# A fixed list of expert units: 42 of 256 rows, or 31 of 256 rows with 12 of 128 rows

## The reference, cut to what matters

```python
h = x @ down_w + down_b
logits = x @ router_w + router_b - COST_LAMBDA * cost
topv, topi = jax.lax.top_k(softmax(logits), 2)
gate = softmax(topv)
for k in range(2):
    mask = one_hot(topi[..., k], 8)
    acc = 0
    for e, (w1, b1, w2, b2) in enumerate(expert_params):
        hm = h * mask[..., e:e + 1]
        acc = acc + (gelu(gelu(hm) @ w1 + b1) @ w2 + b2)
    out = out + acc * gate[..., k:k + 1]
out = out + 0.1 * shared_expert(h); out = out @ up_w + up_b + gelu(x) @ core_w + core_b
```

## Time and profile before

| | |
|---|---|
| median of 3 runs | 737.02 us (733.06 to 739.28) |
| span of the profiled execution | 740.6 us |
| PE busy | 687.7 us, 93% of the span |
| DVE, ACT, POOL busy | 526.1, 541.0, 479.4 us |
| DMA packets | 123.98 MB |
| expert loop, first to last matmul of a unit | 480.01 to 701.34 us |

### The profile page before, as it was taken

One profiled execution on the slowest core, in us unless ns is written; L12 is line 12 of the kernel. 1 busy time (PEld: TensorE's weight loads), 2 busy tenths in 40 slices (PEclk: granted clock), 3 DMA queues, 4 the chain that ended last, 5 costly groups with the idle time before them and its releaser, 6 DMA issues.

```text
span 740.6 us, 20875 instructions
## 1 busy us (share of the span) xinstructions
PE 687.7 (93%) x6101; PEld 373.9 (50%) x6101; DVE 526.1 (71%) x855; ACT 541.0 (73%) x1129; POOL 479.4 (65%) x474
## 2 busy tenths in 40 slices
PE   1799988999999999999999889799999999999998
PEld 0122222323333333223355444488888888888844
DVE  4999998999999999998887746534444444444456
ACT  2399988999999999999895656376666767676511
POOL 3558788888888888986477142135666656566732
PEclk9999999999999999999999989999999999999999
DMA  6555666566665666545355634489987888887487
GB/s 209 190 157 189 197 195 205 176 201 219 205 193 192 207 208 216 176 139 181 97 170 176 208 117 145 155 169 168 142 123 116 122 121 120 101 109 98 57 268 259
DMA packets 136993, 123.98 MB, mean 167 GB/s; under 512 B 70612, under 2 KB 106452, under 8 KB 136920
## 3 DMA queue, kind: packets, MB, share of 16 engines
q1 hardware_dynamic: 122056, 106.58, 50.7%
q0 software_dynamic: 13632, 15.47, 14.9%
q10 hardware_dynamic: 1232, 0.98, 0.4%
HBM read 60.33 MB, written 51.53 MB: 151 GB/s over the span
## 4 chain that ended last, share of the span: by engine, by line
PE 72%; DVE 9%; DMA 6%; issue 5%; ACT 3%; POOL 2%; SPq 1%; another core or an unknown queue 1%; ACTq 0%; DVEq 0%; POOLq 0%
PE EH L1309 24%; PE Y L1309 16%; PE pv L562 13%; PE ring L549 9%; DVE mx L708 6%; PE nat L537 5%; ACT P L633 2%; DMA k_scratch<-khl 1%; PE ring L581 1%; DVE statx L689 1%; POOL y_sums L2136 1%; PE ring L572 1%; SPq L396 1%; DMA rd<-den_scratch 1%
## 5 line engine op out<-in xcount | busy, mean ns | idle before, releaser
L708 DVE TENSOR_REDUCE mx<-nat 128x2 f32<-128x1024 f32 x256 | 296.7, 1214 | 24.0 <-PE nat L537 23.1
L633 ACT ACTIVATE P<-ring 128x512 f32<-128x512 f32 x512 | 279.4, 603 | 20.4 <-PE ring L549 10.5
L2136 POOL DMA_INDIRECT y_sums<-ysb,to x84 | 138.2, 1645 | 100.5 <-DVE ysb L2070 86.7
L562 PE MATMUL pv<-P,VT 128*32 128x256 f32 x2048 | 159.0, 395 | 0.4
L537 PE MATMUL nat<-KS,QS 48*128 48x512 f16 x512 | 111.7, 397 | 25.7 <-DMA QS<-q_scratch 15.6
L549 PE MATMUL ring<-QS,KS 49*128 49x512 f16 x512 | 123.5, 392 | 8.4 <-ACT P L633 8.4
L1673 ACT ACTIVATE X<-EH,bcur 128x256 f32<-128x256 f32 x168 | 85.6, 560 | 50.5 <-DVE u L2024 26.0
L1309 PE MATMUL Y<-whi,u 128*128 x672 | 117.1, 273 | 0.3 <-DVE u L2024 0.3
L1309 PE MATMUL EH<-XA,whi 128*128 128x256 f16 x672 | 116.9, 273 | 0.3 <-DMA XA<-g_rows 0.3
L2024 DVE TENSOR_TENSOR u<-X,u 128x512 f16<-128x512 f32 x84 | 57.8, 688 | 77.1 <-ACT u L1679 76.4
L1309 PE MATMUL EH<-XA,wlo 128*128 128x256 f16 x336 | 91.6, 273 | 0.0
(11 more groups left out here) (267 smaller groups left out, 985.1 us busy)
## 6 DMA issues: line engine op xcount, KB each, us to landing
XA<-in_wall SPq DMA_DIRECT2D x8, 800.0 KB, 4.4
u<-in_wall SPq DMA_DIRECT2D x8, 800.0 KB, 4.4
QS<-q_scratch SPq DMA_DIRECT2D x64, 96.0 KB, 2.6
KS<-k_scratch SPq DMA_DIRECT2D x62, 96.0 KB, 2.3
X<-in_x SPq DMA_DIRECT2D x16, 256.0 KB, 2.9
q_scratch<-qhl SPq DMA_DIRECT2D x16, 256.0 KB, 2.1
xr<-in_x SPq DMA_DIRECT2D x16, 256.0 KB, 3.6
rd<-den_scratch SPq DMA_DIRECT2D x16, 256.0 KB
```

The source lines that it names most:

```text
L562: m = pe.matmul(pv[32 * j:32 * j + 32, q], VT[i][:, lb, g, j, :], Pb[4 * (s % 2) + j][:, q], start=(lb == 0 and half == 0), stop=(lb == 3) ...
L633: act.activation(Pb[4 * (s % 2) + j][:, :], bank[:, :], ACT.Exp).then_inc(t_use.sem, 1)
L708: dve.tensor_reduce(mx[:, k // 8, :, k % 8], nat[k % 2][:, :, :], AX.X, ALU.max).then_inc(t_max.sem, 1)
L2136: pool.indirect_dma_start(out=ysum[:, :], out_offset=bass.IndirectOffsetOnAxis(ap=to[:, j % 2, a:a + 1], axis=0), in_=ysb[j % 2][:, a, :], ...
```

## The change

The list becomes 31 units of 256 rows and N_HALF = 12 units of 128 rows, NJ = 43; the 12 stand at places 2, 5, 8, ... 35 of the order (SMALL). An expert whose count in 128s is odd has its last 128 rows in a small unit. The tables are looked up over 16 classes (8 experts' odd 128s, then 8 experts' 256s) in place of 8. What isn't needed of the small units is used for pieces of pairs, so that the list still suffices for every distribution. The blank rows behind a count are 128 and not 256.

```diff
-NJ = (2 * ROWS // BLK + E - 1) * 2 - HALVES.count(1)
+N_HALF = sum(HALVES)
+N_FULL = ((2 * ROWS // P + E - 1) * 2 - HALVES.count(1) - N_HALF) // 2
+NJ = N_FULL + N_HALF
+SMALL = [2 + 3 * k for k in range(N_HALF)]
+NCL = 2 * E
...
-    tables = ["nf", "ni", "nb", "H", "c1", "c2", "c3", "ex", "dx", "A", "M1", "r1", "M2", "r2", "pki", "D", "valid",
-              "e", "h", "t", "f", "b", "sub", "ro0", "ro1", "ro2", "ro", "wo0", "wo", "bo0", "bo"]
+    tables = ["ni", "no", "nb", "S", "c1", "c2", "c3", "c4", "ex", "q", "q31", "cv", "cvp", "qh", "qo", "qm", "cd", "yA", "yB", "cp",
+              "A", "M", "r", "valid", "pki", "e", "h", "t", "f", "v", "D", "b", "sub", "ro0", "ro1", "rop", "ro2", "ro",
+              "wo0", "wo", "bo0", "bo"]
...
-                (cur(R_(tables[1:7])) if last else []) + old([("core", 1)]) + (cur(R_(tables[7:])) if last else []) + old([("core", 2)])
+                (cur(R_(tables[1:9])) if last else []) + old([("core", 1)]) + (cur(R_(tables[9:])) if last else []) + old([("core", 2)])
...
-                    sp.dma_start(blocks(region[bass.ds(v, BLK), :]), blank).then_inc(t_zr.sem, 16)
+                    sp.dma_start(region[bass.ds(v, P), :], blank[:, 0, :]).then_inc(t_zr.sem, 16)
...
+            if j in SMALL:                      # hidden
+                g = gS[j % 4]
+                wait(pe, t_act, "E", j - 2, 0)
+                for tile in range(4):
+                    for k in range(2):
+                        wc = bass.ds(v + (C_W1 + tile * LAT + k * P), P)
+                        m = three(EH[j % 2][:, 0, tile * P:(tile + 1) * P], wc, g[:, k, :], g[:, 2 + k, :], k == 0, k == 1)
...
+            if j in SMALL:                      # output
+                wait(pe, t_ah, "E", j, 0)
+                wait(pe, t_dve, "E", j, 0)
+                for tile in range(4):
+                    wc = bass.ds(v + (C_W2 + tile * LAT), LAT)
+                    m = three(EY[j % 2][:, 0, :], wc, ah[j % 2][:, tile, 0:P], al[j % 2][:, tile, 0:P],
+                              tile == 0, tile == 3, swap=True, skip=True)
...
+                if j in SMALL:                  # ScalarE
+                    for tile in range(4):
+                        m = act.activation(af[j % 2][:, tile, 0:P], EH[j % 2][:, 0, tile * P:(tile + 1) * P], ACT.Gelu,
+                                           bias=bcur[:, j % 2, tile:tile + 1], scale=bcur[:, j % 2, 4 + tile:5 + tile])
+                    act.copy(ah[j % 2][:, :, 0:P], af[j % 2][:, :, 0:P]).then_inc(t_ah.sem, 1)
...
+                if j in SMALL:                  # VectorE
+                    dve.tensor_tensor(al[j % 2][:, :, 0:P], af[j % 2][:, :, 0:P], ah[j % 2][:, :, 0:P], ALU.subtract).then_inc(t_dve.sem, 1)
+                    collect(j - 1)
...
-                for a, part in enumerate(("half", "y")):
+                for a, part in enumerate(("half", "y")[0:parts(j)]):
```

More of the change, by code:

```diff
@@ L63 @@
 ROWS = B * D
-REGION = ROWS + BLK
+REGION = ROWS + P
 DUMP = E * REGION
@@ L1077, in ffn @@
     SPLIT = NJ - 2
+    assert all(k < SPLIT for k in SMALL) and N_HALF <= 2 * N_FULL
+    parts = lambda j: 1 if j in SMALL else 2
     def plan_sum(tally, j):
@@ L1087, in ffn @@
         t_mt[j % 4].plan(j)
-        t_ad[j % 2].plan(j, n=2)
-        for n in range(2):
+        t_ad[j % 2].plan(j, n=parts(j))
+        for n in range(parts(j)):
             t_act.plan("E", j, n)
@@ L1280, in rest @@
             assert not xloads
-            wait(sp, t_pe, "E", NJ - 1, "h", 1)
+            wait(sp, t_pe, "E", NJ - 1, "h", parts(NJ - 1) - 1)
             for s in ((NJ - 2) % 2, (NJ - 1) % 2):
@@ L1441, in hidden @@
                 if j >= 2:
-                    wait(pe, t_act, "E", j - 2, n)
+                    wait(pe, t_act, "E", j - 2, min(n, parts(j - 2) - 1))
                 elif n == 0:
@@ L1833, in route @@
             if what == "ex":
-                own("c3")
-                return dve.tensor_tensor(csum[:, :], hc[:, 3, 8:16], hc[:, 0, 8:16], ALU.subtract)
+                own("c4")
+                return dve.tensor_tensor(cx[:, :], hc[:, 2, NCL:2 * NCL], hc[:, 0, NCL:2 * NCL], ALU.subtract)
+            if what == "q":
+                own("c4")
+                return dve.tensor_scalar(qi[:, 0, :], kota, n_tails, 0.0, ALU.subtract, ALU.max)
+            if what == "q31":
+                return dve.tensor_scalar(tr[:, 3, tails], kota, n_tails, float(N_FULL), ALU.is_ge, ALU.mult)
@@ new lines, in route @@
+            if what == "cv":
+                own("ex")
+                return dve.tensor_tensor(cv[:, 1:1 + E], cx[:, 0:E], hc[:, 0, NCL + E:2 * NCL], ALU.subtract)
+            if what == "cvp":
+                return dve.tensor_copy(cv[:, 1 + E:1 + NCL], cx[:, E:NCL])
+            if what == "qh":
+                own("q")
+                return dve.tensor_scalar(qi[:, 1, :], qi[:, 0, :], 1, None, ALU.logical_shift_right)
+            if what == "qo":
+                return dve.tensor_scalar(qi[:, 2, :], qi[:, 0, :], 1, None, ALU.bitwise_and)
@@ new lines, in route @@
+            if what == "qm":
+                own("q31")
+                return dve.scalar_tensor_tensor(out=tr[:, 4, tails], in0=kota, scalar=n_tails, in1=tr[:, 3, tails], op0=ALU.min, op1=ALU.add)
+            if what == "cd":
+                own("cvp")
+                return dve.tensor_tensor(cd[:, :], cv[:, 1:1 + NCL], cv[:, 0:NCL], ALU.subtract)
+            if what == "yA":
+                return dve.tensor_scalar(yv[:, pairs], cs2[:, K2_J:K2_J + N_FULL], n_tails, None, ALU.add)
+            if what == "yB":
+                own("qm")
+                return dve.tensor_tensor(yv[:, tails], tr[:, 4, tails], qi[:, 1, :], ALU.add)
@@ L1874, in route @@
+            if what == "v":
+                return dve.tensor_scalar(ti[:, 2, :], ti[:, 0, :], 2 ** V_BITS - 1, None, ALU.bitwise_and)
+            if what == "D":
+                own("v")
+                return dve.scalar_tensor_tensor(out=ti[:, 1, :], in0=yv[:, :], scalar=float(V_BASE), in1=ti[:, 2, :],
+                                                op0=ALU.add, op1=ALU.subtract)
             if what == "b":
@@ L1889, in route @@
                                                 op0=ALU.mult, op1=ALU.add)
+            if what == "rop":
+                own("ro1")
+                return dve.scalar_tensor_tensor(out=tr[:, 1, tails], in0=qi[:, 2, :], scalar=float(P), in1=tr[:, 1, tails],
+                                                op0=ALU.mult, op1=ALU.add)
             if what == "ro2":
-                own("ro1")
+                own("rop")
                 own("valid")
```

175 lines of the change are left out of this document (101 added, 74 removed).

## The result

| | before | after |
|---|---|---|
| median of 4 runs | 735.81 us (733.06 to 739.28) | 715.62 us (711.88 to 716.37) |
| ratio | | 0.9721, 95% interval 0.9675 to 0.9767 |
| span of the profiled execution | 740.6 us | 714.4 us |
| expert loop, first to last matmul of a unit | 480.01 to 701.34 us, 221.3 | 480.15 to 675.14 us, 195.0 |

The change saves 20.2 us at the median (17.1 to 23.9 by the interval), and 26.2 us between the two profiled executions. The profiled execution of before is not one of the four that were timed: its span alone, 740.6 us, is above the slowest of them, 739.28, though a time is some 1.9 us longer than its span (716.26 and 714.4 us in the execution after). I had said 710.4 us, in a range of 705 to 719; it took 715.62, so the direction and the range hold, and the centre is off by 5.2 us.

A forecast was written before the change was run, and what follows sets the result against it. PE was taken to bound the loop, the other engines waiting for it. Loop -26.1, tables +1.5 and blank-row writes -2 made -26.6 us: 737.0 - 26.6 = 710.4 us, range 705 to 719.

The forecast's parts named there:

- The loop: PE's expert loop: 31 full units of 5.24 us and 12 small of 2.63 make 194.0 us, saving 26.1 us.
- The price of a narrow matmul: Small unit's hidden on PE: 128-column matmuls at 0.055 us each, 24 in 1.32 us; at 0.09 us, 16.0 us saved.
- The other engines: ACT, DVE, POOL and DMA in the loop: none becomes the bound; `to` holds by 0.25 us; cost 0.
- The second cover: In the loop, behind the 0.25 us of slack at DVE's `to`, PE has 1.3 us more.
- The tables: DVE's table operations ahead of the loop, on the path through `sal` and `ro`: +1.5 us, from 1.0 to 2.9.
- The blank rows: Blank-row writes ahead of the loop: half the burst gives back part of DVE's 6.51 us idle, 0 to 4, taken -2.
- behind the loop: After the expert loop nothing changes, since the last seven units (36 to 42) are full.
- A: Rival: narrow matmuls in the loop don't halve but take 0.08 to 0.09 us; loop saves 16 to 18, 720 us; chance 0.13.
- B: Rival: small stalls at each small unit in the loop; each 0.5 us costs 6 us, with 1 us 722; chance 0.10.
- C: Rival: the scatter's return becomes the loop's clock, slower than before, 744 us or more; chance 0.02.
- D: Rival: a wait behind the loop for POOL's last DMA to land takes the gain; no separate chance given.

The follow-up runs named there:

- the later sessions: Changed kernel run again against the kernel before, on other chips: 700.45 us against 726.49 (ratio 0.9656), then 701.42 against 726.05 (0.9666).
- the empty wait: Changed kernel with three idle reductions on DVE ahead of `sal`, so PE waits 6.83 us: 709.89 us against 726.2 of the kernel before, 0.9789.

## Why the prediction was right, and where it was off

**The loop: right.** Predicted 194.0 us for the units and 1.2 of start-up, 195.2; measured 195.0 in the first comparison and 196.2 to 196.9 in the later traces of this order without an added wait. The start-up is the difference: where the loop starts early, its first gelu waits for `xb_rows`, and the first small unit's hidden takes 1.89 to 2.06 us, against 1.70 in the first comparison. The price of a narrow matmul was the main doubt, and the eight transposes of the earlier trace rows gave it to 2%: 24 narrow matmuls take 1.34 us, where 1.32 was forecast. By the rule of the Trainium skill that I had weighed (TensorE: Matmul & The Clock Gate, Back-to-back issue gap: 81 ns at 128 columns), hidden would take 1.94 us, an estimate; the trace has 1.34 in the stream, and 2.1 to 2.2 for small units in a row. The loop's first pair of loads, 0.09 us apart, has the pace that the small units in a row show. My reason, that PE's stream runs ahead during wide matmuls, fits both orders; what the runs show is that the price depends on the order.

**The other engines: right, with one term mis-sized.** A gelu of 128 columns: 0.4 us forecast; four of them take 1.51 us. `to` was said to hold by 0.25 us; it waits about 1 us at twelve places. One of them, in the timeline after, unit 10's sum on DVE, the second of its two DMAs on POOL, and `to(12)` on DVE:

```profile
519.25 0.68 DVE L2163 TENSOR_TENSOR ysb<-Y,gcur 128x512 f32<-128x512 f32 x1
...
522.08 2.07 POOL L2229 DMA_INDIRECT y_sums<-ysb,to  x1 [0.30 <-DMA y_sums<-ysb,to]
...
528.36 0.17 DVE L2151 TENSOR_SCALAR to<-meta 128x2 uint32<-128x2 f32 x1 [1.72 <-DMA y_sums<-ysb,to]
```

Unit 10 is full, unit 11 small, and `to(12)` waits for the scatter of unit 10: the pair that I had priced. From the sum to the second DMA it is 2.83 us (forecast 3.03), and DVE was free for `to` at 526.64, 7.4 us after the sum (forecast 7.6). What was mis-sized is the landing: `to` starts 6.3 us after the second DMA did, where I took 4.32 from the last DMA behind the loop and not from one in it. The longest landing in the view of `y_sums` is 5.7 us after the change, 5.0 before. Why a landing is longer here was not taken apart. The second cover, PE's 1.3 us, held: its matmuls sat idle 0.1 us in the loop.

**The tables: right on DVE, less than that on the path elsewhere.** Core sum 1 to `bo`: 6.32 to 7.67, +1.35 for a forecast of +1.5. Its parts: in front of the comparison 1.14 less 0.19, so +0.95 (forecast 1.1 with the two gone taken off); the wide passes from five to three, 2.58 to 2.60, so 0.0 (+0.1); behind them +0.4 (+0.3). The forecast's 5.75 and 7.3 us count from the first operation of the tables to core sum 2; so counted it is 5.75 to 7.09. In the later sessions only +0.8 to +1.0 reaches the loop's start, because before, PE's own chain is what comes last there and hides part.

**The blank rows: wrong.** -2 us was taken, from a correlation in time: the gap of 6.5 us on DVE ended with the last write. Half the rows shortened the writes by 1.1 to 1.2 us in each place (13.66 to 12.49, 9.80 to 8.69) and the start of core sum 1 by 0.1. What the gap is stays open. It stands in both traces of the first comparison, PE's instructions show gaps called "issue" in it, and none of the later traces has it, with 128 or with 256 blank rows.

**A step that was missing: what the longer wait does to the clock.** I put the wait for `sal` at 2.83 + 1.3 us and priced it as time on the path, no more. PE was idle for 4.15 us there, the granted clock fell to one half and 28 products took 2.7 us longer. The earlier trace rows show the wait that the tables lengthen, and rows on 437 to 444 us of the same trace (shown above) already had the price: 3.52 us idle, then matmuls 0.21 us apart. That was to be had before the change was run. In the later sessions the wait is 0.65 us and the term is absent. Not all of the 2.7 us is a loss at the end: with the loop 2.5 to 2.7 us late for another reason, 0.6 to 1.1 us were left, since ScalarE's first step would have waited for `xb_rows` (the earlier trace rows have this wait, and I priced nothing by it). If the same share holds in the first comparison, which no run shows, the clock cost about 1 us of time there, and the rest stands as a shorter start-up in the loop's -26.3.

**The sum, put right.** Loop -26.3, tables +1.3, clock +2.7, blank rows -0.1, behind the loop 0: -22.4 us for the first comparison, whose medians differ by 20.2. In the later sessions: loop -25.0, start +1.0, so -24.0, measured -24.6 and -26.0. The saving at the median fell 6.4 us short of the sum (26.6 against 20.2). The blank rows' -2, of which -0.1 came, and the clock's +2.7 make 4.6 of them; the loop and the tables came out 0.4 better than forecast; the other 2.2 are within the interval of the ratio (17.1 to 23.9). The 5.2 us at the median are less than the 6.4, because the base, 737.0, was 1.2 above the later median.

**The rivals.** A fell at this order and is true of small units in a row. B and C fell: TensorE's idle time in the loop is 0.1 us. D fell: the last landing is 4.71 us where it was 4.32, and the first product behind it comes 10.3 us after the loop's end where it was 9.9.

## What to carry to other kernels

A matmul with half the columns cost half here only between wide ones; put narrow pieces between wide ones, one in three here, and count the cover of every buffer for the pair that comes closest together, with the longest landing of the loop and not one from its end. When the chain names a releaser, look in the kernel whether the instruction really needs that one. When an edit lengthens a wait ahead of a dense stretch on TensorE, look in the trace for what the granted clock did after other waits of that length, and price the matmuls behind it at both levels; then look for the next wait behind them, which may hide part of it. And before a span is used as the base of a sum, look whether that one execution carries a stall of its own.

## What the runs showed of the hardware

- The same 24 matmuls of 128 columns with addresses from a register: 1.34 us (0.056 each) between full units, 2.1 to 2.2 us (0.09 each) from the third small unit of a row on, at a granted clock of 1.00 in both.
- Idle times of PE ahead of the `y` products and the granted clock after them: 0.65 us, up; 2.83 us, up; 3.52 (in the group before), 4.15 and 6.83 us, down to one half. After 2.02 us idle it fell too, 0.5 us into the products. So the length of the one wait alone does not tell it.
- The low stretch of the clock made the 28 products ahead of the loop 2.7 us longer in the first comparison and 2.1 with the empty wait. Executions of one kernel spread by about as much: the changed kernel took 699.77 and 700.45 us at a mean clock of 1.0 and 700.35 to 703.12 at 0.997.
- Eight blank-row writes were issued in 12.5 to 13.7 us in one place and 8.7 to 9.9 in the others, with a stall of 6 us on DVE beside the first and none beside the second. Why is open.
- A scatter-add of 128 rows into `y_sums` landed after 1.9 us at least, 2.9 in the median and 5.7 at most; one in mid-loop let DVE go on 6.3 us after POOL had started it, the last one behind the loop 4.7.
